# P times V over whole tiles with a block diagonal P, moved behind the key transposes of a recurrent plus local-attention kernel

## The reference, cut to what matters

```python
xn = layernorm(x)                                     # x: [2, 1024, 128]
s = recurrent_block(xn)                               # gated linear recurrence, 192 channels
for i in range(6):                                    # DEPTH
    xn = attn_layer(shift_tokens(xn), Wqkv[i], q_scale[i], k_scale[i], Wo[i]) + xn
    xn = ffn_layer(shift_tokens(xn), ln_g[i], ln_b[i], W1[i], b1[i], W2[i], b2[i]) + xn
out = x + s * silu(xn)

def attn_layer(x, Wqkv, qs, ks, Wo):                  # 16 heads of 64, windows of 32
    q, k, v = heads(x @ Wqkv)
    q, k = rotary(l2norm(q) * qs), rotary(l2norm(k) * ks)
    # each query sees its own window of 32 keys and the one before, masked to a band
    p = softmax(masked(8.0 * q @ k.T))                # [b, h, window, 32, 64]
    return merge_heads(p @ v) @ Wo
```

## Time and profile before

| | |
|---|---|
| median of 3 runs | 1976.27 us (1963.19 to 1985.96) |
| profiled execution | 1975.02 us |
| its span | 1972.9 us |
| mean granted clock of TensorE | 0.921 |
| busy: PE / weight loads / DVE / ACT / POOL | 84% / 72% / 71% / 60% / 62% |
| instructions recorded | 76065, of them 32303 matmuls and 32303 weight loads |

### The profile page before, as it was taken

The page is one execution under the profiler, slowest core; times in us unless marked ns, Lnnn a source line. Parts: engine busy times, 40 slices in busy tenths (PEclk is TensorE's granted clock), DMA queues, the critical chain, the costliest instruction groups (busy, mean ns, idle before and its releaser), DMA issues.

```text
span 1972.9 us, 76065 instructions
## 1 busy us (share of the span) xinstructions
PE 1659.1 (84%) x32303; PEld 1428.6 (72%) x32303; DVE 1408.8 (71%) x2215; ACT 1190.2 (60%) x2318; POOL 1218.6 (62%) x1085
## 2 busy tenths in 40 slices
PE   6888888888888888888888988888888878888886
PEld 4677777777777767776777777777777767767775
DVE  7787777777766777677777767667777776766645
ACT  5566566566565656666665766566567565655543
POOL 7766676666666666567666657656567655555520
PEclk8899999999988999899999989989899998898978
DMA  3343233333323333232343322334233222222221
GB/s 101 91 110 83 59 85 71 89 96 81 73 64 80 93 81 95 63 79 60 90 110 73 82 69 69 77 88 102 61 74 78 72 66 63 59 56 55 51 70 47
DMA packets 217855, 151.19 MB, mean 77 GB/s; under 512 B 144556, under 2 KB 164656, under 8 KB 217520
## 3 DMA queue, kind: packets, MB, share of 16 engines
q1 hardware_dynamic: 217520, 146.33, 30.5%
HBM read 27.50 MB, written 1.05 MB: 14 GB/s over the span
## 4 chain that ended last, share of the span: by engine, by line
PE 62%; DVE 20%; issue 13%; ACT 2%; POOL 1%; DMA 0%; SPq 0%; DVEq 0%; POOLq 0%; ACTq 0%
PE ps_pv L870 12%; PE ps_pv L903 8%; PE ps_s L844 7%; PE ps_tr L791 6%; PE ps_qn L779 6%; DVE t L1485 6%; DVE qk L1488 5%; PE ps_qn L781 5%; PE ps_qn L780 5%; PE ps_pv L883 3%; DVE rsum L1527 3%; PE ps_tr L804 3%; DVE normal L1755 2%; ACT sq L1144 2%; DVE ss L1498 1%
## 5 line engine op out<-in xcount | busy, mean ns | idle before, releaser
L1960 POOL TENSOR_TENSOR qk<-qk,t 128x1024 f32<-128x1024 f32 x192 | 457.6, 2384 | 326.9 <-DVE qk L1488 326.9
L1485 DVE TENSOR_TENSOR t<-ps_qn,tab 128x512 f32<-128x512 f32 x384 | 262.3, 683 | 303.4 <-ACT sq L1144 303.0
L779 PE MATMUL ps_qn<-w_hi,xs_hi 128*128 128x512 f32 x576 | 293.0, 509 | 100.3 <-DVE qk L1488 95.7
L1972 POOL TENSOR_TENSOR qkr<-qk,rinv 128x1024 f32<-128x1024 f32 x192 | 361.3, 1903 | 7.5
L870 PE MATMUL ps_pv<-pT,v_win 64*64 64x32 f32 x12288 | 237.2, 227 | 127.6 <-issue 122.6
L870 PEld LDWEIGHTS ps_pv<-pT,v_win 64*64 64x64 f32 x12288 | 217.9, 143 | 147.8 <-issue 142.2
L1144 ACT ACTIVATE sq<-ps_qn 128x512 f32<-128x512 f32 x384 | 230.2, 600 | 105.3 <-PE ps_qn L781 93.0
L1488 DVE TENSOR_TENSOR qk<-ps_qn,tab 128x512 f32<-128x512 f32 x384 | 260.4, 678 | 0.0
L779 PEld LDWEIGHTS ps_qn<-w_hi,xs_hi 128*128 128x128 f32 x576 | 119.4, 207 | 179.5 <-issue 97.7
L780 PE MATMUL ps_qn<-w_lo,xs_hi 128*128 128x512 f32 x576 | 247.8, 430 | 1.9 <-issue 1.9
L781 PE MATMUL ps_qn<-w_hi,xs_lo 128*128 128x512 f32 x576 | 247.2, 429 | 0.7 <-issue 0.7
(11 more groups left out here) (165 smaller groups left out, 3171.9 us busy)
## 6 DMA issues: line engine op xcount, KB each, us to landing
v_win<-v_new SPq DMA_DIRECT2D x576, 128.0 KB, 2.4
v_win<-v_new SPq DMA_DIRECT2D x192, 64.0 KB, 2.0
v_win<-v_win SPq DMA_DIRECT2D x188, 64.0 KB, 2.0
kT<-kT SPq DMA_DIRECT2D x84, 128.0 KB, 2.8
w_raw<-in_Wqkv SPq DMA_DIRECT2D x18, 512.0 KB, 4.3
rot<-in_rot SPq DMA_DIRECT2D x48, 128.0 KB
wo<-in_Wo SPq DMA_DIRECT2D x6, 512.0 KB, 4.2
x<-x SPq DMA_DIRECT2D x48, 56.0 KB
```

The source lines that it names most:

```text
L779: mm(ps_qn[bank][:, :], xs_hi[b][:, :], w_hi[:, part], start=True, stop=False)
L1485: v.tensor_tensor(t2[:, part].rearrange("p (h s d) -> p h s d", s=2, d=DH // 2), swapped, tab[:, 2 * k + 1:2 * k + 2, :].rearrange("p o (s ...
L1960: g.tensor_tensor(qk[b][:, part], qk[b][:, part], t2[:, part], ALU.add).then_inc(added[b], 1)
L1972: g.tensor_tensor(qkr[b][:, part].rearrange("p (h d) -> p h d", d=DH), qk[b][:, part].rearrange("p (h d) -> p h d", d=DH), rinv[b][:, k * ...
```

## The change

P times V. P is written into a tile `pbd` of twice the size, in which the 64 rows of the one head and those of the other stand in different columns and the rest is zero (set once at the start). One matmul then takes all 128 rows (two heads), 64 columns of weights and 2 x 32 moving columns. There are 32 matmuls (64 records) a half step instead of 64 (128). Each fills 64 partitions of one bank, alternating between the lower and the upper 64. ACT writes `pbd` in two pieces of 64 rows per bank.

Order. P times V moves from the end of the half step to behind the key transposes; the scores are the last PE work of a half step. The mask and the transpose of the next input move behind projections 2 and 3; the transposes of the FFN rows become a fill of their own. FFN up 0 and 1 move behind the query transposes. `low_x` and `low_fxn` move from DVE to GpSimd. `inverse_root` moves from the end of ACT's half step to the start of the next, ahead of the copies of P, and the copies of P times V follow the keys'. `xmid` has three slots instead of four. SyncE moves V for stream b in the half step of the same b.

```diff
-MID_RING = 4
+MID_RING = 3
@@ pv_order
-        if b == 0 and valid(i - 4):
-            order += [("up", c) for c in range(3)]
         if valid(i - 2):
-            order += [("pv", b, h) for h in range(2)]
+            order += [("pv", b, f) for f in range(2)]
+        if b == 0 and valid(i - 4):
+            order += [("up", c) for c in range(3)]
@@ layer_tiles
-    w.pT = sb("pT", [P, HP, P])
+    w.pbd = sb("pbd", [P, HP, 2, P])
@@ SyncE half
                     if b == 0:
                         carry_k(i, 1)
-                        move_v(i - 1, 1)
                         shift_xmid(i)
                         load_out_weights(i)
                     else:
                         carry_k(i + 1, 0)
-                        move_v(i, 0)
+                    move_v(i, b)
@@ PE probs_v
+            out = ps_pv[bank][DH * (hp % 2):DH * (hp % 2 + 1), :].rearrange("p (g h w q) -> p g h w q", g=2, h=2, w=WINDOWS)
+            return out[:, hp // 2 % 2, :, w, :]
...
                     for g in (2 * f, 2 * f + 1):
                         for w in range(WINDOWS):
+                            for hp in (2 * g, 2 * g + 1):
+                                last = mm(pv_target(bank, hp, w), v_win[b][:, w, hp * DH:(hp + 1) * DH],
+                                          pbd[:, hp, :, WINDOW * w:WINDOW * (w + 1)], start=True, stop=True)
+                    last.then_inc(pv_full[bank], 1)
@@ PE half
                     out_projection(i, 1 - b)
-                    if b == 0:
-                        ffn_up(i, 0)
                     transpose_keys(i, b)
-                    mask(i, b)
+                    probs_v(i, b, 0)
+                    probs_v(i, b, 1)
                     qkv(i, b, (2, 3))
...
+                    transpose_mixed(i, b)
+                    mask(i, b)
                     rec_hidden(i, b)
                     rec_gate_projection(i, b)
-                    if b == 0:
-                        ffn_up(i, 1)
...
                     transpose_qk(i, b, 1)
+                    if b == 0:
+                        ffn_up(i, 0)
+                        ffn_up(i, 1)
                     qkv(i, b, (4, 5))
...
                         ffn_up(i, 2)
-                    if not i.first:
-                        transpose_mixed(i, b)
+                    else:
+                        transpose_rows(i)
                     scores(i, b, 0)
                     scores(i, b, 1)
-                    probs_v(i, b, 0)
-                    probs_v(i, b, 1)
@@ ACT evac_probs
-                    f(pT[:, 4 * k:4 * k + 4, :].rearrange("p m t -> p (m t)"), ps_tr[bank][:, :], ACT.Copy).then_inc(tr_done[bank], 1)
+                    for h in range(2):
+                        rows = slice(DH * h, DH * (h + 1))
+                        last = f(pbd[rows, 4 * k:4 * k + 4, h, :], ps_tr[bank][rows, :].rearrange("p (m t) -> p m t", m=4), ACT.Copy)
+                    last.then_inc(tr_done[bank], 1)
@@ ACT half
-                    evac_pv(*before(i, b), 0)
-                    evac_pv(*before(i, b), 1)
+                    inverse_root(*norm_tile(i, b), i - 3)
                     evac_probs(i, b, 0)
...
                     evac_k(i, b, 1)
+                    evac_pv(i, b, 0)
+                    evac_pv(i, b, 1)
                     square(i, b, 2)
+                    evac_mixed(i, b)
                     square(i, b, 3)
@@ DVE half
                     if b == 0:
                         ffn_gate(i, 0)
-                        ffn_gate(i, 1)
...
-                    if not (i.first and b == 0):
+                    if (i.n, b) in ((0, 1), (1, 0)):
                         low_x(*next_tile(i, b))
                     if b == 0:
+                        ffn_gate(i, 1)
+                        ffn_gate(i, 2)
                         mid_variance(i)
-                    else:
-                        low_fxn(i - 3)
@@ GpSimd half
                     scale(s, other, 1)
+                    if b == 0:
+                        low_fxn(i - 4)
                     scale(s, other, 0)
                     add(i, b, 0)
...
                     scale_probs(*softmax_tile(i, b))
+                    if i.n > 1 or (i.n, b) == (1, 1):
+                        low_x(*next_tile(i, b))
                     add(i, b, 1)
```

173 lines of the change are left out of this document (87 added, 86 removed).

## The result

The changed kernel takes 1765.45 us (median of 4 runs, 1763.68 to 1767.49); the kernel before took 1981.12 us beside it (1963.19 to 1988.25, with the runs shown above). The ratio is 0.892, 95% interval 0.886 to 0.899. The forecast was 1860 us with a range of 1785 to 1945: the direction is right, the size is not. The time is outside the range, next to the first rival ("the chain alone decides", 1788 us, chance 0.15).

The account below looks back on a forecast made before the run. Neither engine full: PE and DVE take turns, with instruction-fetch stops in P times V on the path. Between -3.9 (chain) and -1.8 (PE) it took -2.4 us a step, times 48: 1975 - 115 = 1860 us, range 1785 to 1945.

Parts of the forecast that it names:

- the first rival: The chain of waits alone sets the gain, 3.9 us for each of 48 steps: 1788 us; chance 0.15.
- the stops: PE's unexplained waits in P times V, 122.6 us in 91 pieces, taken as PE outrunning its instruction fetching.
- the handover: End of a half step: P times V, 3.48 us at b = 0, stands on the path before the next q projection.
- The price of the new form: P times V on PE: 92 ns a record in its half, 3.5 us a half step, +1.0 us of PE.
- the slower rival: P times V's column halves do not overlap: 5.9 us a burst in a quick stretch, 2160 us; chance 0.09.
- the floor in step 4: PE, at 17.4 us of work and 96% busy, keeps the half step from going below 18.1 us.
- The third rotation of b = 0: Start of VectorE's second rotation pair: PE's work upstream of it changes by -1.7 us.
- The gate's new wait: VectorE's first gate product in b = 0 waits for the gelu moved later: 0.9 us of idle time.
- The wait at VectorE's low part: A 1.62 us wait in VectorE's queue before statistics and maxima, to go with the low parts on GpSimd.
- The 0.5 us on the second rotations: ScalarE writes P in two pieces; the second delays the second square, 0.5 us on each half's second rotation.
- The sum: Per step, the chain gives -3.9 us and PE's floor -1.8; -2.4 taken, times 48 steps is 115 us.
- the mixture of the two that I called my own: The prediction's own case, between chain and PE's floor at -2.4 us a step: 1815 to 1910 us, chance 0.57.

Follow-up runs that it names:

- e8: The changed kernel with every product of P times V issued twice: 1875.83 us, ratio 0.953.
- e1: The changed kernel with P times V in its old form (64x64 quarters, single copy of P) at the new place: 1844.11 us, ratio 0.940.
- e6: The changed kernel with P times V behind the scores again, new form kept: 1822.62 us, ratio 0.926.
- e3: The changed kernel with only the low parts back on VectorE: 1772.82 us, ratio 0.902.
- e9: e6 with FFN up 0 and 1, their gelus and gates and the low parts back where they were: 1811.29 us, ratio 0.911.
- e12: e9 with the input's transpose and its copies at the end of the half step again: 1848.92 us, ratio 0.945.
- e7: The changed kernel with each of the first two squares on ScalarE ahead of the copy of P that stood before it: 1780.96 us, ratio 0.905.
- e4: The changed kernel with the mask's two matmuls issued twice: 1761.12 us.
- e2: The kernel before with only the new form of P times V, still behind the scores: 1881.74 us, ratio 0.958.
- e5: The kernel before with four repeats of the mask ahead of the value projections of b = 1: 1978.88 us, ratio 1.004.
- e14: The changed kernel with only the normalisation of the rows moved to GpSimd: 1745.32 us, ratio 0.886.

## Why the prediction was wrong

Step by step, in the prediction's order.

1. **What bounds the kernel, and the stops.** Right on the stops: they were PE outrunning its instructions. 89 of 90 end behind the landing of a packet, and e8 has as many records in P times V as e1 and almost no stops, at half the rate. The changed kernel's instruction queue moved 211 packets, 47 fewer; from 100 to 1600 us PE still has 20 stops over 0.3 us that are put down to issue, 48 us, where it had 84 and 114. Half right on the handover: with the new form the place is worth 57 us (e6), and it shows in b = 1, not in b = 0 whose 3.48 us the step had named.
2. **The price of the new form.** The column halves overlap, so the slower rival (5.9 us a burst) is out. But a pair takes 73 ns and not 92, and in e8's longer bursts 62: most of the load that I had left uncovered is covered. I then scaled by 2.44 / 2.07 to 3.5 us, and had +1.0 us of PE a half step. Measured are 214.4 / 96 = 2.2 us, 0.2 less than before; the whole group is busy 214.4 us where I had said near 330. This term was mis-sized, and the floor in step 4 rested on it.
3. **The moves.** The third rotation of b = 0 was to come 1.7 us earlier: it is 1.6 (10.9 to 9.3). The gate's new wait was to be 0.9 us: 0.87. The wait at VectorE's low part was to go and did, for another reason than given (e3, e9, e12): the step credited GpSimd, and the early transpose did it. The 0.5 us on the second rotations is there in the rows (0.3), and e7, which takes it away, gains nothing by it.
4. **The sum, the step that failed.** The chain was to give 3.9 us a step. Measured, by the mean intervals between 300 and 1250 us, are 38.1 - 34.3 = 3.8 us; half by half 2.5 in b = 0, where the maxima were to come 2.6 earlier, and 1.3 in b = 1. Over the whole program the two means fell from 19.0 and 20.5 to 17.1 and 17.9, 4.5 us a step, and 48 times that is the 215 us seen; the sum never looked at the two ends, so that a chain of 3.9 us gives 1788 and not 1765. I then took 2.4, because "PE's work goes from 16.4 to 17.4 us" and "at 96% of the same clock, the half step cannot be below 18.1". It is 17.0. What failed is the work: it is 15.4 us and not 17.4, since the form costs no PE time (2.26 us a half step against 2.44) and the records are shorter at the clock granted now (0.983 against 0.921), the projections alone by 0.8 us a half step. By the same rule 15.4 us give a floor of 16.1, under the 17.0 that were measured, and it would have capped nothing; e4 agrees, with more PE work at no cost. The 96% itself is not refuted: no run passed 95%, which e8 reached with 760.10 us of 800. A floor made of PE's busy time before carried the clock of the kernel before and a mis-sized term.

What the chances were worth: the case that came had 0.15, and its only argument against it was that same floor. It should have had more than the mixture of the two that I called my own.

## What to carry to other kernels

A floor from an engine's busy time holds only for the work as it will be: reckon it again with the new form and the clock that it will be granted, and test it by issuing something cheap twice before letting it cap a chain that is worked out from waits. A wait in an engine's queue can be ended by making its input earlier; moving the waiting operation to another engine may then add nothing. And a share of the chain is not a price: ScalarE's copies of P held 8% of it, and putting the squares ahead of them made the kernel slower.

## What the runs showed of the hardware

- Stops of PE's instruction supply follow the rate of records, not their number: 41.1 us of stops for 12288 records at 16 ns each, 2.4 us for 12288 at 31 ns, in the same place, with 258 packets on the instruction queue both times. They end 1.2 to 1.8 us after a packet of 16 KB has landed (89 of 90 in the kernel before). Behind the scores (12 to 16 ns a record) the new form has them too, 32.9 us in e2 and 37.5 in e6. The Trainium skill ("Runtime: NRT & Kernel Launch", Instruction fetch mechanics) calls the crossing of a block mostly hidden; by these runs that holds for a burst at 31 ns a record that stands alone and fails at 16.
- Float32 records with all 128 rows, 64 columns of weights and 64 moving columns, issued to the two column halves in turn, run at 62 (e8) to 73 ns (changed kernel) a pair, their weight loads included.
- VectorE's normalisation, which reads and writes SBUF alone, takes 0.34 us with no GpSimd record beside it (5 records of the changed kernel) and 1.43 us on average when one runs as it begins (87); all of these 87 end 0.08 or 0.09 us after that GpSimd record does. In the usual pair they take 1.00 us and 1.94, the second behind a GpSimd product of 1.91 us. The maxima, which read PSUM, take 1.21 to 1.23 us, 92 of 96 beside GpSimd. The Trainium skill ("SBUF — State Buffer", SBUF: two separate sides) says that the pair of ports that both engines use is locked for a whole instruction and that the other engine blocks, for VectorE work in a two-port mode or with two SBUF inputs. The pairs agree with it; that the normalisation runs in such a mode no view here shows. Moving the two records to GpSimd was worth 20 us (e14).
- Filling PE's idle stretch raised the mean granted clock from 0.921 to 0.943 (e5); the time did not fall, with the filler's own cost in it.
